# A four-layer graph network on one core: where the conv table is built and where the pair scatters are issued

## The reference, cut to what matters here

```python
def spline_conv(x, row, col, basis, idx, W, b):
    z = jnp.einsum('ni,kio->nko', x, W).reshape(N * K, Fout)     # the "table", K = 125 kernels per node
    gathered = z[col[:, None] * K + idx]                         # 8 rows of it per edge
    msg = jnp.einsum('es,eso->eo', basis, gathered)
    out = jax.ops.segment_sum(msg, row, num_segments=N)
    ...
# layer 0: h = elu(conv1(1)); h = elu(spline_conv(h, ..., stn2)); t = linear layers(h)
#          pseudo' = clip(pseudo + t[dst] - t[src], 0, 1); out = spline_conv(x, ..., conv_w)
# last layers: sums over edges, done as products with an adjacency matrix of edge counts
```

## Time and profile before

| what | value |
|---|---|
| median of 2 runs | 11371.64 us (11367.02 to 11376.25) |
| profiled execution: span of its instructions | 12824.6 us |
| profiled execution: time of its own beside the span | none is given |
| instructions | 84,874 |
| busy: PE, DVE, ACT, POOL | 27%, 42%, 19%, 53% of the span |
| stn2 sweep (z_stn gathers) | about 2871 to 5182 us of the span |
| stage with the targets | about 5383 to 6453 us |
| conv sweep (z_conv gathers) | about 6502 to 7580 us |

### The profile page before, as it was taken

How to read it: one execution, slowest core, us unless ns; L and a number is a source line. 1 busy time by engine, 2 the same in 40 slices (tenths; PEclk the granted TensorE clock), 3 DMA queues, 4 the chain that set the end, 5 groups by cost and what they waited for, 6 DMA issues and landing times. The chain is left out here.

```text
span 12824.6 us, 84874 instructions
## 1 busy us (share of the span) xinstructions
PE 3493.7 (27%) x19713; PEld 2186.6 (17%) x19713; DVE 5436.1 (42%) x7001; ACT 2482.3 (19%) x3625; POOL 6756.2 (53%) x6784
## 2 busy tenths in 40 slices
PE   4344201763333333303500010001000100005877
PEld 3222101331111111302500000001000100004544
DVE  5333485444454444303754442222222377773111
ACT  0222152432222222101200001111111134430000
POOL 2666475006666666573057767776777566661000
PEclk8555555985555555556755555555555555557899
DMA  6000021877777777200046641111111123335799
GB/s 272 2 3 3 12 106 63 345 295 230 240 238 231 238 233 233 64 0 0 0 134 188 176 108 36 34 33 27 36 33 33 26 73 93 95 98 186 320 386 360
DMA packets 587391, 1693.59 MB, mean 132 GB/s; under 512 B 268075, under 2 KB 322770, under 8 KB 569201
## 3 DMA queue, kind: packets, MB, share of 16 engines
q0 software_dynamic: 292720, 608.23, 18.6%
q1 hardware_dynamic: 230560, 722.30, 14.5%
q10 hardware_dynamic: 63952, 361.30, 7.6%
HBM read 1016.07 MB, written 675.24 MB: 132 GB/s over the span
## 5 line engine op out<-in xcount | busy, mean ns | idle before, releaser
L1997 POOL DMA_INDIRECT ring<-tab_gat,at x2352 | 2347.4, 998 | 928.3 <-issue 835.5
L724 POOL DMA_INDIRECT ring<-z_stn,at x1568 | 1514.8, 966 | 1506.8 <-POOLq L721 991.1
L724 POOL DMA_INDIRECT ring<-z_conv,at x784 | 794.3, 1013 | 853.9 <-POOLq L721 592.9
L1517 PE MATMUL pair_acc<-pair_w,pair_cell 32*112 32x384 f32 (+1 forms) x1120 | 806.0, 887 | 1499.7 <-issue 468.9
L578 POOL DMA_INDIRECT sorted<-rows,at x784 | 800.8, 1021 | 710.6 <-POOLq L576 477.3
L1100 POOL DMA_INDIRECT adj<-val_a,at_a x784 | 785.5, 1002 | 335.0 <-issue 255.7
L2576 PE MATMUL acc<-spot,ones 128*128 128x128 f32 x6 | 2.3, 487 | 3444.1 <-PEq L1965 2243.5
L1267 PE MATMUL acc<-tile,parts 128*96 128x448 f16 (+1 forms) x3430 | 728.5, 361 | 254.4 <-DVE parts L1191 139.2
L1916 DVE COPY corner_banks<-w 128x56 f32 (+1 forms) x140 | 35.7, 255 | 1549.5 <-issue 389.7
L2108 DVE COPY peak<-peak 128x6 f32<-128x6 f32 x112 | 21.4, 191 | 1567.3 <-DMA ring<-tab_gat,at 1521.1
L1517 PEld LDWEIGHTS pair_acc<-pair_w,pair_cell 32*112 32x112 f32 x1120 | 307.8, 295 | 1996.9 <-issue 1996.9
(11 more groups left out here) (510 smaller groups left out, 9794.9 us busy)
## 6 DMA issues: line engine op xcount, KB each, us to landing
tile<-adj SPq DMA_DIRECT2D x490, 784.0 KB, 21.4
z_stn<-block ACTq DMA_DIRECT2D x245, 800.0 KB, 4.9
z_conv<-pair_block ACTq DMA_DIRECT2D x224, 700.0 KB
run_gat<-out_rows SPq DMA_DIRECT2D x56, 1596.0 KB
adj<-zero SPq DMA_DIRECT2D x49, 1568.0 KB
run_basis<-out_rows SPq DMA_DIRECT2D x28, 1750.0 KB
ring<-tab_gat,at POOLq DMA_INDIRECT x2352
run_gat<-out_rows SPq DMA_DIRECT2D x56, 672.0 KB
```

What stands on the lines that cost most here:

```text
L724: g.indirect_dma_start(out=view(bufs[b], k), out_offset=None, in_=table, in_offset=bass.IndirectOffsetOnAxis(ap=at[n][b][:, k:k + 1], axis ...
L1517: last = pe.matmul(self.acc[g][0:self.nodes, n, 0:(hi - lo) * self.fo], self.cell[:, :], cols, start=True, stop=True)
L1997: g.indirect_dma_start(out=ring[b][:, k, :], out_offset=None, in_=tab_gat, in_offset=bass.IndirectOffsetOnAxis(ap=at[b][:, k:k + 1], axis= ...
```

## The change

1. `PairTable` leaves `summed_sweep`. It is built anew inside `stage_targets`: 49 tiles of 128 nodes, 7 tiles per loop step of four halves. PE transposes the 7 tiles of x once a step and issues the planes after the `look` of each unit, 35 planes on 28 units (`planes_after`: one plane each, two on every fourth). ACT copies a plane to its block right after the cast of the unit. There is one PSUM buffer for planes (`pair_acc`, two banks) in place of two, and one for `turned` in place of two. The two matmuls of a plane use partitions 0 to 31 and 32 to 63. SP issues the stores.
2. `stage_targets` has no POOL work any more. `hot_hi` is compared from `digits` in SBUF; the copy to `keys` in PSUM (L1779) goes.
3. The stn2 sweep gets 7 pair scatters per step: after every second column's two gathers one scatter, 4 in chunk 0 and 3 in chunk 1. DVE copies the indices and values of the next step's scatters to small tiles at the end of each chunk, after a wait on the last step's scatters.
4. The basis sweep scatters the second 392 columns in place of the first.

```diff
@@ summed_sweep @@
+                                    if scatter and k % 2 == 0 and k // 2 < some[b]:
+                                        if k == 0:
+                                            g.wait_ge(sem(f"pairs_staged{b}"), 1)
+                                            g.sem_inc(sem(f"pairs_staged{b}"), -1)
+                                        g.indirect_dma_start(
+                                            out=adj, out_offset=bass.IndirectOffsetOnAxis(ap=pair_at[b][:, k // 2:k // 2 + 1], axis=0),
+                                            in_=pair_val[b][:, k // 2:k // 2 + 1], in_offset=None).then_inc(sent[b].sem, 16)
...
-                            if pairs:
-                                pairs.scalar(a, it, 3 * b, 3 + 2 * b, True)
...
+                            if scatter:
+                                v.wait_ge(sent[b].sem, it * (16 * some[b]) + (16 * some[b] + sent_base[b]))
...
+                                stage_pairs_of(b, it * ch + (ch + b * some[0]))
@@ PairTable @@
+            def tensor_plane(self, pe, n):
+                k, plane = divmod(n, KD)
+                pe.wait_ge(sem("planes_free0"), 1)
+                pe.sem_inc(sem("planes_free0"), -1)
+                for m, (lo, hi) in enumerate(self.pieces):
+                    rows = slice(m * self.kin, (m + 1) * self.kin)
+                    cols = self.wsb[rows, plane, 0:hi - lo, :].rearrange("i k o -> i (k o)")
+                    pe.matmul(self.acc[:, m, 0:(hi - lo) * self.fo], self.turned[rows, k, :], cols,
+                              start=True, stop=True).then_inc(sem("plane_for_act"), 1)
...
+            def scalar_plane(self, a, it, n):
+                k, plane = divmod(n, KD)
+                if plane < self.n_blocks:
+                    a.wait_ge(self.stored[plane].sem, it * (16 * TB) + (16 * k + self.start[plane]))
...
+                a.wait_ge(sem("plane_for_act"), 2)
+                a.sem_inc(sem("plane_for_act"), -2)
+                for slot in range(2):
+                    if 0 <= plane - slot < self.n_blocks:
+                        for m, (lo, hi) in enumerate(self.pieces):
+                            last = a.copy(self.blocks[plane - slot][:, lo:hi, slot, :], ...)
...
+                a.sem_inc(sem("planes_free0"), 1)
+                if plane > 0:
+                    a.sem_inc(sem("pair_block_full"), 1)
@@ stage_targets, ScalarE @@
+                        for n in range(4 * units):
...
+                            a.copy(lo_rows[b][:, u * UN:(u + 1) * UN, :], turned[:, :, :]).then_inc(act_step, 1)
...
+                            a.sem_inc(sem("lo_rows_ready"), 1)
+                            if n == 0:
+                                pairs.scalar_turned(a)
+                                a.sem_inc(sem("z_tiles_ready"), 1)
+                            for m in planes_after(n):
+                                pairs.scalar_plane(a, it, m)
@@ stage_targets, TensorE @@
                             turn(b, 0)
-                            for u in range(1, units):
-                                turn(b, u)
+                            if half == 0:
+                                pairs.tensor_turn(pe)
+                            for u in range(1, units + 1):
+                                rows_taken()
+                                if u < units:
+                                    turn(b, u)
                                 look(b, u - 1)
...
+                                for m in planes_after(half * units + u - 1):
+                                    pairs.tensor_plane(pe, m)
@@ program @@
-                                     lambda g: scatter_pairs(g, at_a, val_a, 0, J // 2))
+                                     lambda g: scatter_pairs(g, at_a, val_a, J // 2, J))
```

More of the change, by code:

```diff
@@ L713, in summed_sweep @@
                 per = 16 * ch * len(gathers)
+                if scatter:
+                    at_a, val_a = scatter
+                    some = [ch - ch // 2, ch // 2]
+                    pair_at = [sb(st, f"pair_at{b}", [P, some[b]], I32) for b in range(2)]
+                    pair_val = [sb(st, f"pair_val{b}", [P, some[b]], F16) for b in range(2)]
+                    sent = [counted(f"pairs_sent{b}") for b in range(2)]
+                    sent_base = [k.base for k in sent]
+                    for b in range(2):
+                        sent[b].base += 16 * some[b] * steps
                 @block.gpsimd
@@ L813, in _ @@
                     v.sem_inc(sem("decay_cleared"), 1)
+                    if scatter:
+                        for b in range(2):
+                            stage_pairs_of(b, b * some[0])
                     for b in range(2):
@@ L1491, in sync @@
[L1491 to L1521, removed]
@@ new lines, in __init__ @@
+                self.pieces = [(0, KD * KD // 2), (KD * KD // 2, KD * KD)]
+                most = max(hi - lo for lo, hi in self.pieces)
+                self.wsb = sb(st, "pair_w", [2 * kin, KD, most, fo])
+                self.acc = ps(st, "pair_acc", [P, 2, 512])
+                self.stored = [counted(f"z_stored{a}") for a in range(self.n_blocks)]
+                self.weights_on = [self.stored[plane % self.n_blocks] for plane in range(KD)]
+                self.start = [k.base + 16 * 2 * self.weights_on.count(k) for k in self.stored]
@@ L1738, in stage_targets @@
                 moved = sb(st, "moved", [P, J, D3])
-                keys = ps(st, "keys", [P, 512])[:, 0:CH]
+                pairs = PairTable(st, *z_args)
+                planes = TB * KD
                 counts_ = ps(st, "counts", [P, 512])[:, 0:NT]
-                turned = [ps(st, f"turned{b}", [P, UN, P]) for b in range(2)]
+                turned = ps(st, "turned", [P, UN, P])
                 found = [ps(st, f"found{b}", [P, UN, 256]) for b in range(2)]
-                @block.gpsimd
-                def _(g):
-                    pool(g)
                 @block.vector
@@ L1894, in _, with stage_spline_sweep @@
                     table.scalar(a)
-        def stage_spline_sweep(z, fo, starts, w8, keep, run, tail, ch, table=None):
+        def stage_spline_sweep(z, fo, starts, w8, keep, run, tail, ch, scatter=None):
             with ExitStack() as st:
@@ L1905, in stage_spline_sweep @@
                 wgt8 = banks[:, used:used + ch * 8].rearrange("p (j s) -> p j s", s=8)
-                pairs = PairTable(st, *table) if table else None
                 def produce(v, b, col, sums):
@@ L1943, in stage_spline_sweep @@
                 views = [whole] if paired else [plane(0), plane(1)]
-                summed_sweep([(z, at, ring, view) for at, view in zip(starts, views)], ch, fo, produce, run, keep, tail, pairs=pairs)
+                summed_sweep([(z, at, ring, view) for at, view in zip(starts, views)], ch, fo, produce, run, keep, tail, scatter=scatter)
         def node_sums(st, run, end_i, open_, tail, width):
```

192 lines of the change are left out of this document (101 added, 91 removed).

## The result

The changed kernel takes 12,771.6 us (12,769.1 to 12,774.1), the kernel before 11,371.6 us: the ratio is 1.1228 [1.1196 to 1.1261], so the change is slower, by 1,400 us. The profiled execution took 12,774.1 us for a span of 12,772.3.

What follows compares the result with a forecast made beforehand. POOL's issuing was taken to bound the stn2 sweep. 11371.6 + 460 (scatters in the sweep) + 875 (planes in the targets stage) = 12,707, said as 12,700 us; range of 8 in 10: 11,960 to 13,020.

Steps and rivals of the forecast that it cites:

- Stn2 sweep, +460: Stn2 sweep: 392 added scatters at POOL's pace of 1.25 us make 490 us; taken as +460.
- Basis sweep, 0: Basis sweep: the same number of scatters as before, so no change.
- Targets, planes, +875: Targets stage: 245 planes on 196 units, PE's and ACT's parts adding up; 1450 us against 575, so +875.
- the slow level of the clock: Targets stage: with TensorE's clock near 0.50, 7.9 us a unit, 1560 us; at the fast level 6.1 us, 1205.
- the crawl: Targets stage while POOL scatters (505 us): PE's matmuls 2.8 us apart, no engine named for the wait.
- The drain at a change of tiling: Targets stage: changing tiling mode drains TensorE, twice a unit; no size given, spoke for the slow end.
- Conv sweep and later, 0: Conv sweep and everything later: unchanged, 0.
- The crawl is the cost of recording, four to one: Unnamed pauses in targets, stn2 sweep and attention come from profiling, explaining 985 of 1453 us; four times as likely as not.
- Planes that don't overlap: Rival, targets stage: a plane's two matmuls do not overlap on PE, 370 us more, 13,070 us; chance 0.09.
- The crawl is real: Rival: targets takes 1070 us in runs now, the sweep's pauses absorb scatters (+230); 11,980 us; chance 0.13.
- Faster: Rival: without POOL's scatters in targets, planes slip in beside DVE's work, stage near 650 us; 11,090 us; chance 0.05.

Runs made afterwards that it cites:

- later_planes_scatters_in_z: Changed kernel with ACT copying planes after the next unit's cast and the second 392 scatters in the stn2 table's stage: 11,854.4 us, ratio 1.041.
- scatters_in_z: Kernel before with the second 392 pair scatters moved from the targets stage to the stage building the stn2 table: 11,397.3 us, ratio 1.0023.
- before_third: Kernel before, unchanged, profiled again on chip 3: 12,875.5 us.
- planes_a_unit_later: Changed kernel with ACT copying a unit's planes after the next unit's cast: 13,186.4 us on chip 7 (1.0222), 13,203.3 on chip 3 (1.0264).
- before_again: Kernel before, unchanged, profiled once more on chip 7: 12,869.7 us, timed runs beside it 12,877.

## Why the prediction came out, point by point

- *Stn2 sweep, +460.* Right, by the mechanism given. In the two traces of one chip it is +477, and in the first result's trace the sweep has 2510 us. The scatters take 395.3 + 119.4 = 515 us of POOL, 1.31 us each and not 1.25 (they are 1.01 us long, a gather 0.97); given back are some 56 us of pauses between gathers (issue, 501.8 to 445.9). I had 490 less 30, the 30 for the DMA load of the table's stores. That reason was wrong, and its size came out by luck: in later_planes_scatters_in_z, whose sweep has neither stores nor scatters, these pauses are 519.3 us and the sweep is 2040 us, 9 less than with the table. The pauses shrink where scatters stand between the gathers; why, no run shows.
- *Basis sweep, 0.* Right: its 392 scatters span 514 us, the same in both kernels.
- *Targets, planes, +875.* Right in mechanism, and small by 68 us. For the unit shown I would have 7.2 us (with 1.68 for the copies); it is 6.98, as turn and look took 2.22 for my 2.08, the plane 1.76 for my 1.4, and the hand-overs and waits 0.74 for my 1.45. Over the stage it is 1472 / 196 = 7.5 us a unit, where I had 7.9 at the slow level of the clock and chose 7.4 between (1450 / 196); the granted clock of the stage was 0.52, the slow level. So two errors met: the slow unit was 0.4 us cheaper than I had it, and the clock slower than I had it. That the stage ended at 1472 for my 1450 is in part luck. The rest of the 68 is on the side of before: I took 575 us for its stage, from the period of a half, and without the crawl it is 530.
- *The drain at a change of tiling* (the Trainium skill, TensorEngine Tiling (Array Packing), section Key Properties) can be bounded here: PE's first weight load for the plane begins at 6007.98, 0.23 us after the look's last and with no releaser, and the plane's matmuls begin with it, 0.07 us before the modelled end of the look's. A drain is no more than these 0.23 us, 45 us over 196 units, an estimate from this one unit; whether they are a drain no run shows. The slow end was reached for the clock's sake.
- *Conv sweep and later, 0.* Right: on chip 13 the conv sweep takes 1023 us in the changed kernel and 1022 in scatters_in_z, attention 3386 and 3384.
- *The crawl is the cost of recording, four to one.* This was the wrong step, though the time that came of it was right, and that was luck: the timed runs of before and the changed kernel's both came from the state without the crawl (the sort takes 1059 us in the trace after). Where the crawl is, the same change would come to a ratio of about 1.06 (below). Timed runs of before take 12,877 and 12,875 us on two chips, where traces show the crawl, and on two others it is in neither. The shown profile of before came from the one state and its shown runs from the other; that is why a span of 12,824.6 stood beside runs of 11,371.6, and recording does not make the difference: the profiled execution of scatters_in_z took 11,405.5 us, its nine others 11,382.1 to 11,409.3, and that of before_third 12,875.5 beside runs of 12,875. The first sentence that I quoted from the Trainium skill (NOTIFIC — the notification-queue block, section 10: an implicit record costs the engine nothing) agrees with this, and the back-pressure of its section 7.1 does not explain the difference, as traces with the same number of instructions stand in either state. What did hold was the arithmetic: taking the stages without the crawl for runs of 11,371. I had 495 us for it in the targets and 270 in the sweep; it is 511 and 274.
- *Rivals.* Planes that don't overlap: priced at 370, measured at 310 when forced, and not the case. "The crawl is real" has its truth on chips 7 and 3, but not in its base, which is 12,877 and 12,875 there and not 11,372, and not in its terms: the sweep +377 for its +230, the targets stage from 1043 to 1470, +427 for its +380. That gives 12,877 + 377 + 427 = 13,680 us for the changed kernel there, an estimate from planes_a_unit_later, before_again and the changed kernel's stage, and a ratio of 1.06 for the 1.05 of that rival. *Faster* needed less than 4.4 us a unit; even with the planes a unit later it is 972 / 196 = 5.0, or 4.9 on chips 7 and 3, where that version is 2.2 and 2.6% over before.

## What to carry to other kernels

Work that rides in a stage bound by another engine is nearly free there (9 us for the table, 65 with the crawl), and its price elsewhere is not its busy time but its place in the order: two engines with one buffer between them add up, and a copy moved behind the next hand-over won back 500 of 943 us. When a profile's span and the timed runs differ much, here by an eighth, compare first whether both come from the same state of the chip: run the unchanged kernel again, and take each stage's length from a trace whose span agrees with the runs.

## What was not expected of the hardware

- The same program takes 11,371 to 11,383 us on chips 13 and 8 and 12,875 to 12,877 on chips 7 and 3, with equal durations of its instructions. The difference is longest where POOL issues indirect DMAs, one in 1.27 us, beside the other engines: 511 us of the targets stage, in which PE stands up to 67 us at a time with no releaser (before_third). It is not there where these engines have the stage to themselves (532 us on chip 3), nor in the basis sweep, where POOL scatters as well (514 us on either kind of chip). What makes the state is not settled: I can tell neither whether it is the chip's own or that of a sitting, nor why the basis sweep is spared, nor what the engines wait for; whether their own instructions reach them late wasn't tested.
- The two 32-row matmul pieces of a plane (four records, 384 or 416 f32 columns) take PE 1.76 us on two row groups, 3.03 us on one, at a granted clock of 0.52 and 0.50.
- A scatter of 128 two-byte elements from the small tiles of the sweep is 1.01 us long on POOL, from the large tile of all values 0.97, each with 0.30 us before the next.
